# Two graph layers on one core: in layer 1 the projection of v, its eviction and its residual part are moved within each row

## The reference, cut to what matters

```python
h = relu(layernorm(x))
q, k, v = split_heads(h @ Wq), split_heads(h @ Wk), split_heads(h @ Wv)   # 4 heads of 64
sim = einsum('bhid,bhjd->bhij', q, k) * scale
attn = softmax(where(adjacency_mask, sim, neg))
out = einsum('bhij,bhjd->bhid', attn, v)
x = x + (merge_heads(out) @ Wo + bo)
```

## Time and profile before

| | us |
|---|---|
| median of 3 runs | 2652.82 (2652.71 to 2655.8) |
| the profiled execution, its own time | 2656.29 |
| its span, first to last instruction | 2654.5 |
| mean granted clock of PE over the span | 0.994 |
| PE busy | 2587.7 (97%) |
| DVE busy | 1990.9 (75%) |
| ACT busy | 1754.5 (66%) |
| POOL busy | 1399.6 (53%) |

### The profile page before, as it was taken

One profiled execution on the slowest core, in us unless ns is written; L12 is line 12 of the kernel. 1 busy time (PEld: TensorE's weight loads), 2 busy tenths in 40 slices (PEclk: granted clock), 3 DMA queues, 4 the chain that ended last, 5 costly groups with the idle time before them and its releaser, 6 DMA issues. The chain is left out here.

```text
span 2654.5 us, 62516 instructions
## 1 busy us (share of the span) xinstructions
PE 2587.7 (97%) x20882; PEld 1393.6 (52%) x20886; DVE 1990.9 (75%) x6361; ACT 1754.5 (66%) x5020; POOL 1399.6 (53%) x2790
## 2 busy tenths in 40 slices
PE   6999999999999999999999999997999999999998
PEld 3455555555555555555555555554555555555554
DVE  6477778777877777777777777786777777777766
ACT  3566666666666666666666666675777777777774
POOL 4255545545554555555555555544565656555552
PEclk9999999999999999999999999998999999999999
DMA  5367766776667666766776677678786777778774
GB/s 141 61 136 158 144 135 133 149 155 130 145 141 140 145 128 144 149 142 133 141 147 141 131 140 146 148 141 195 158 175 160 169 163 170 164 160 170 158 149 102
DMA packets 945489, 387.43 MB, mean 146 GB/s; under 512 B 857617, under 2 KB 859153, under 8 KB 945169
## 3 DMA queue, kind: packets, MB, share of 16 engines
q1 hardware_dynamic: 945168, 383.44, 69.0%
HBM read 114.86 MB, written 67.11 MB: 69 GB/s over the span
## 5 line engine op out<-in xcount | busy, mean ns | idle before, releaser
L552 ACT ACTIVATE probs<-probs,negmax 128x128 f32<-128x128 f32 x1024 | 398.2, 390 | 455.6 <-DVE negmax L124 455.6
L465 POOL TENSOR_TENSOR o_sb<-o_sb,xres 128x512 f32<-128x512 f32 x127 | 161.5, 1272 | 496.5 <-DVE o_sb L739 493.1
L166 PE MATMUL l_ps_pj<-hT,room 128*128 128x512 f16 x1488 | 346.7, 383 | 2.3 <-ACT room L1343 2.3
L166 PE MATMUL ps_pj<-wm_hi,hT 128*128 128x512 f16 x1024 | 326.4, 380 | 12.6 <-DVE wm_lo L761 6.8
L166 PE MATMUL ps_pj<-wv_hi,hT 128*128 128x512 f16 x1024 | 326.4, 380 | 0.0
L166 PE MATMUL ps_pj<-hT,wk_hi 128*128 128x512 f16 x1024 | 305.9, 380 | 0.0
L166 PE MATMUL ps_pj<-hT,wq_hi 128*128 128x512 f16 x1024 | 304.5, 379 | 0.0
L1357 ACT ACTIVATE l_probs<-l_probs,l_negmax 128x128 f32<-128x128 f32 x512 | 199.2, 390 | 139.0 <-DVE l_negmax L124 138.8
L1292 POOL TENSOR_TENSOR l_h<-l_h 128x512 f16<-128x512 f32 x120 | 139.6, 1164 | 282.3 <-DVE l_out_sb L1440 245.0
L124 DVE CUSTOM_DVE_ANT_0 probs<-ps_sc,mask 128x128 f32<-128x128 f32 x1024 | 235.4, 285 | 47.4 <-PE ps_sc L981 46.7
L721 DVE SCALAR_TENSOR_TENSOR c<-cprobs,c 128x512 f16<-128x512 f32 x256 | 185.2, 723 | 79.6 <-ACT c L559 79.2
(11 more groups left out here) (172 smaller groups left out, 6198.8 us busy)
## 6 DMA issues: line engine op xcount, KB each, us to landing
xg<-in_x SPq DMA_DIRECT2D x128, 256.0 KB, 3.4
xres<-in_x SPq DMA_DIRECT2D x128, 256.0 KB, 3.1
x_scratch<-o_sb SPq DMA_DIRECT2D x128, 256.0 KB, 2.4
out<-l_out_sb SPq DMA_DIRECT2D x128, 256.0 KB, 3.3
l_ring<-x_scratch SPq DMA_DIRECT2D x124, 256.0 KB, 3.2
mask_u<-in_adj SPq DMA_DIRECT2D x64, 64.0 KB, 2.8
cpT<-c SPq DMA_TRANSPOSE x256, 3.2
xg<-x_scratch SPq DMA_DIRECT2D x12, 256.0 KB, 3.2
```

The source lines that it names most:

```text
L166: last = pe.matmul(out, a(kt), b(kt), start=(n == 0), stop=(n == 3 * kts - 1))
L465: nc.gpsimd.tensor_tensor(o_sb[:, j % 2], o_sb[:, j % 2], xres[:, j % 2], ALU.add).then_inc(res_done, 1)
L552: last = nc.scalar.activation(probs[:, i], probs[:, i], ACT.Exp, bias=negmax[:, u % 2, i:i + 1], scale=-1.0, accum_out=zsum[:, u % 4, hh:h ...
```

## The change

In each pass, `project_v(n+4)` goes from behind `scores(n+1)` to right behind `project_qk(n+4)` on PE; `v_high(n+4)` goes from behind `exps(n+1)` to ahead of it on ACT; `v_low(n+4)` goes from behind `normalise(n+1)` to the head of the pass on DVE. No instruction is added or taken away and no wait is changed. `weigh_values(n-2)` stays last on PE and so follows `scores(n+1)`.

```diff
@@ ACT @@
                     relu(n + 10)
                     h_high(n + 10)
+                v_high(n + QUAD)
                 exps(n + 1)
-                v_high(n + QUAD)
                 if n >= 2:
                     aT_high(n - 2)
                 p_high(n + 1)
@@ DVE @@
             for n in range(B - QUAD):
+                v_low(n + QUAD)
                 if n >= 4:
                     add_residual(n - 4)
                 row_max(n + 1)
                 if n + 15 < B:
                     stats(n + 15)
                 normalise(n + 1)
-                v_low(n + QUAD)
                 if n >= 2:
                     aT_low(n - 2)
                 p_low(n + 1)
@@ PE @@
                 project_qk(n + QUAD)
+                project_v(n + QUAD)
                 if n >= 4:
                     project_out(n - 4)
                 scores(n + 1)
-                project_v(n + QUAD)
                 if n >= 2:
                     weigh_values(n - 2)
```

## The result

The changed kernel takes 2773.24 us (median of 4 runs, 2771.4 to 2775.84), the one before 2654.06 (4 runs). The ratio is 1.0449, with a 95% interval of 1.0431 to 1.0467: 119 us slower. The forecast was 2766, or +112.

What follows compares the result with a forecast made beforehand. PE, busy throughout at 6.51 us per pass, bounded the kernel; a 7.47 us chain of waits through ACT and DVE would replace it. Terms 109 - 2 + 5 = +112 us gave 2766 us, range 2740 to 2800.

Steps and rivals of the forecast that it cites:

- The circle: ACT and DVE waiting for each other, from `qk_copy` through `v_high`, `v_low`, `exps`, `p_high` to `qk_copy`: 7.47 us, +109 us.
- POOL's share: `normalise` on DVE slowed beside POOL's mask conversion in one pass of four: 5 us, bounds 0 and 27.
- the conversion's tail: Only the end of POOL's mask conversion was counted as overlapping `normalise`, by a few tenths of a microsecond.
- End and start: Passes 118 to 123, without `relu` and `h_high`, catch up 2 us; first four passes 0, some 3 us either way.
- PE's gain: PE's pass getting shorter by its new order: taken as 0, at most 0.2 us per pass.
- The scores' new place: On PE, scores start at about 5.4 instead of 3.99 us of the pass; the 1.41 us lost are on no path.
- an eviction that frees nothing: PE never waited for v's bank, so evicting v earlier gains nothing.
- PE's wait: One PE wait per pass, some 0.9 us before the q/k block, for `qk_copy`; none before v, scores or output.
- my own signs of being wrong: Prediction wrong if `v_low` starts without a wait, the pass is 6.5 us, or an unnamed wait stands in it.
- The circle that does not close: Rival: ACT and DVE overlap enough that PE stays the bound; at most -24 us, 2629, without gain 2653; chance 0.03.
- `add_residual` is held by POOL: Rival on DVE: `add_residual` slowed beside POOL's `h_low`, 0.6 us per pass longer, +68 us, 2834; chance 0.05.
- The falling clock: Rival on PE: idle 0.9 us per pass lowers its clock; +194, 2960, or in one pass of four +48, 2814; chance 0.04.

Runs made afterwards that it cites:

- Two experiments: Against the changed kernel: `add_residual` ahead of `v_low` on DVE, 2697.12 us; `v_high` ahead of `relu` and `h_high` on ACT, 2647.82 us.
- The two variants that open the circle: Against the changed kernel: `v_high` ahead of `relu` and `h_high` on ACT, 2647.82 us; `v_low` behind `row_max` on DVE, 2644.57 us.
- the first experiment: Against the changed kernel, PE back in its old order (v behind the scores), ACT and DVE as changed: 2836.62 us, ratio 1.0686.

## Why the prediction was right, point by point

**The circle.** Shown. Nine steps were read from the trace before as 0.59, 0.83, 0.52, 0.39, 0.34, 0.67, 0.97, 2.62 and 0.54, sum 7.47; the changed kernel's are listed above, sum 7.46. Two experiments take out what they aim at, one step of 0.66 and two of together 1.35 us, and the time follows: 6.78 us per pass in the one, PE's own pass in the other, where the opened circle shows its 6.08 in the passes that catch up. The loss in size: in most passes 7.45 - 6.51 = 0.94, times 114 is 107 us.

**POOL's share.** Right in place, too small in size. I took 5 us of a possible 27. The pass with the conversion is 7.79, so 0.34 longer, 28 times: 9.5 us. (Two more passes took 7.59; their 0.14 stays unexplained.) The overlap is not the conversion's tail alone, since POOL got to it later than I had it: it began at 2223.23, just ahead of the division.

**End and start.** At the fifth copy, the changed kernel is 0.5 us behind, of the 3 that I left open. Passes without `relu` and `h_high` took 6.09 to 6.40 where 6.12 was forecast. From the copies, the changed kernel is 117.9 us behind at pass 118 and 116.5 at pass 123. The two profiled spans differ by 2769.6 - 2654.5 = 115.1, against 119 between the medians: the profiled executions took 2656.3 and 2771.4, which is 2.2 above and 1.8 below the medians.

**PE's gain.** I took 0 and bounded it by 0.2 per pass. It is real, 0.11 per pass: 6.51 before, 6.40 now wherever PE runs without a wait. The circle hides it in the changed kernel. The two variants that open the circle show it, some 11 and 13 us.

**The scores' new place, and an eviction that frees nothing.** Here the text was wrong for the single part, right for the whole. It said that the scores' 1.41 us are not on a path. With PE alone changed they are, at +136 us. That the change as a whole loses less is because `v_low` at DVE's head opens this circle while closing the other. Likewise "an earlier eviction frees nothing that anyone wants" held for the old PE order only: with v behind q/k, PE does want `v_low` early.

**PE's wait.** Wrong. I said one wait of 0.9 us in each pass, before the q/k block, and none before the scores. In four passes it is one of 0.59 to 1.33 us before a q/k block and one of 2.12 before the first scores of a group, and in 13 of 28 groups one more before another q/k block, mostly of 0.9. PE gains 1.05 us per pass on the circle (7.45 against 6.40) until the first scores of a group, which wait for their group's last copy:

```profile
2203.03 0.71 PE L1510 MATMUL l_ps_s<-room 64*128 64x128 f32 x8 [2.12 <-issue]
...
2217.89 2.33 PE L166 MATMUL l_ps_pj<-hT,room 128*128 128x512 f16 x10 [0.89 <-ACT room L1345]
...
2225.69 2.76 PE L166 MATMUL l_ps_pj<-hT,room 128*128 128x512 f16 x12 [1.32 <-ACT room L1343]
...
2233.18 1.03 PE L1510 MATMUL l_ps_s<-room 64*128 64x128 f32 x8 [2.12 <-issue]
```

The copy that the scores at 2203.03 waited for is the one at 2202.26, which ends at 2202.93. I had left this wait out of my list, and it is what surprised me in the first experiment. A wait in the pass that I had not named was one of my own signs of being wrong, and it is there. It touches PE's side of the account, not the circle that sets the pass. In the changed kernel it costs nothing, since nothing of the same pass's circle stands behind it.

**Rivals.** The circle that does not close is refuted for the changed kernel. That `add_residual` is held by POOL is refuted: with the changed kernel it runs beside POOL's `h_low` (2204.37 to 2205.53 there), and its 128 cases are 736 to 752 ns.

```profile
L1440 DVE SCALAR_TENSOR_TENSOR l_out_sb<-l_ps_o,l_w_st,l_xres x128: 736/743/752, 1850.5 to 2766.4; 128x512 f32<-128x512 f32 x128
```

The falling clock is refuted in the form that I gave it, and half right in another. Idle times of 0.9 us did not lower the clock: with PE alone changed, PE waited 0.95 to 1.23 us in each of 114 passes, and the granted clock over the span was 0.994, as before. In the changed kernel it does fall, to a mean of 0.95 to 1.00 in windows of 100 us, and 0.986 over the span, where I had said 1.00. From 1850 to 2700 us every fall came right behind a wait of 2.12 us before the scores, in 15 of 28 groups. There it costs nothing that can be seen: the passes behind a fall are 7.45 too, since PE's slower matmuls fill the time of the third wait, and with the conversion moved, the mean is 0.984 and the passes are still 7.43 to 7.45. In the first experiment it costs, because v stands behind the idle time on PE and ahead of `v_high` on the circle. The Trainium skill (TensorE: Matmul & The Clock Gate, A second HAM failure mode: psum-queue depth-cycling) describes a clock that swings from frequent short idle times between groups of matmuls. The 114 short waits with PE alone changed, at 0.994, showed nothing of the kind; a swinging clock did come here, but behind the longer waits.

## What to carry to other kernels

When an eviction is moved forward on two engines, list what stands ahead of its first half and behind its second half: the move joins these two lists into one chain, and if the chain comes back to its start, its sum of start-to-start distances is the new pass, where it is longer than the pass of the busiest engine. Here the chain summed from the trace before came within 0.02 us of the measured pass. It can be opened by moving one instruction out of it, or back; the instruction behind which `v_low` stands was worth 5% of the whole kernel. And list the waits that stand in only some passes: the one missed here, the first scores of a group for the last copy of that group, stands in one pass of four. Do the sum for each part of an edit by itself as well, since two parts can each close a circle, and one may hide the other's.

## What the runs showed of the hardware that I had not expected

From the start of v's 12 matmuls to their follower it is 1.41 us where the weighted values follow (2213.62 to 2215.03 before), and 1.31 where the output projection does (2206.74 to 2208.05 in the changed kernel). Before, the first weight load of the weighted values came with 0.21 us of idle weight loader ahead of it:

```profile
2208.52 0.14 PEld L1523 LDWEIGHTS l_ps_av<-l_pT,l_v_hi 128*64 128x64 f16 x4 [0.21 <-issue]
```

In the changed kernel the weighted values follow the f32 scores, with no such gap and the same 0.65 us from scores to follower. That is 0.10 of PE's 0.11 per pass. Why the small weights are not loaded ahead there stays open; no run here varied it.

After 3.42 us without a matmul the next 4 us had a granted clock of 0.57, and the scores and v behind it ran at 1.2 GHz in large part. In 7 of 28 passes of the same variant it did not fall after the same 3.42 us (from 2133 to 2141 it was 1.00). After 2.12 us, in the changed kernel, it fell in 15 of 28 groups and not in the others: the scores at 2203.03 took 0.71 us, and those at 2233.18, after the same 2.12, took 1.03. So the length of the idle time alone does not decide it; what does, no run here shows.
